# The reciprocal of the softmax row sums on GpSimd, as a power, in front of its multiply

## What is computed

```python
x = x + _L0_xattn_ref(_layernorm(x), ctx_1024, ctx_1024, mask, Wq, bq, Wk, bk, Wv, bv, Wo, bo)
x = x + _L0_ffn_ref(_layernorm(x), w_gate, b_gate, W1, b1, W2, b2)
# inside the attention:
scores = jnp.einsum('bhqd,bhkd->bhqk', q, k) / jnp.sqrt(jnp.float32(DH))
scores = jnp.where(m, -jnp.inf, scores)
attn = jax.nn.softmax(scores, axis=-1)
ctx = jnp.einsum('bhqk,bhkd->bhqd', attn, v)
# inside the experts: the best of 8 experts per token, by a softmax gate
h = jax.nn.relu(jnp.einsum('nd,edm->enm', x_flat, W1) + b1[:, None, :])
y = jnp.einsum('enm,emd->end', h, W2) + b2[:, None, :]
out = y[route_idx, jnp.arange(n)] * route_p[:, None]
```

## Time and profile before

| | |
|---|---|
| median of three runs | 152.0 us (150.82 to 152.23) |
| the profiled execution's own time | 151.69 us |
| its span, first to last instruction | 150.0 us |
| mean granted TensorE clock | 0.876 |
| TensorE busy with matmuls | 110.7 us |
| VectorE busy | 83.6 us |
| ScalarE busy | 71.2 us |
| GpSimd busy | 51.0 us |

### The profile page before, as it was taken

One profiled execution on the slowest core, in us unless ns is written; L12 is line 12 of the kernel. 1 busy time (PEld: TensorE's weight loads), 2 busy tenths in 40 slices (PEclk: granted clock), 3 DMA queues, 4 the chain that ended last, 5 costly groups with the idle time before them and its releaser, 6 DMA issues.

```text
span 150.0 us, 2810 instructions
## 1 busy us (share of the span) xinstructions
PE 110.7 (74%) x753; PEld 87.5 (58%) x753; DVE 83.6 (56%) x292; ACT 71.2 (47%) x355; POOL 51.0 (34%) x82
## 2 busy tenths in 40 slices
PE   5689865997949995989587670848199899898130
PEld 5558644664746574757465560627198699797130
DVE  0340899675523855685668478277172757676010
ACT  0046451416599229782979420313535386466000
POOL 4004075002222332233274543053303615565411
PEclk9999997899996999999999998555559999999655
DMA  4979999999992000000000001101102323200000
GB/s 136 310 244 305 275 271 251 238 255 377 300 283 97 4 0 0 0 2 4 0 20 18 4 0 38 47 26 38 32 5 75 95 54 75 68 20 18 26 0 9
DMA packets 17610, 15.09 MB, mean 101 GB/s; under 512 B 1256, under 2 KB 14756, under 8 KB 17584
## 3 DMA queue, kind: packets, MB, share of 16 engines
q1 hardware_dynamic: 16384, 12.58, 32.9%
q0 software_dynamic: 672, 1.07, 2.2%
q10 hardware_dynamic: 528, 1.14, 2.2%
HBM read 8.92 MB, written 6.19 MB: 101 GB/s over the span
## 4 chain that ended last, share of the span: by engine, by line
PE 51%; DVE 21%; issue 10%; ACT 8%; POOL 4%; DMA 3%; ACTq 0%; DVEq 0%; POOLq 0%
PE bank L865 10%; PE bank L1009 9%; PE bank L877 8%; PE bank L983 6%; ACT probs L696 5%; PE bank L893 4%; PE bank L994 4%; DVE normed L1238 3%; PE bank L960 3%; DMA mask_u<-in_mask_1xSxS_bk 3%; PE bank L946 2%; POOL probs L548 2%; DVE probs_T L1442 2%; PE bank L980 2%; PE bank L851 1%
## 5 line engine op out<-in xcount | busy, mean ns | idle before, releaser
L696 ACT ACTIVATE probs<-bank,neg_max 128x64 f32<-128x64 f32 x120 | 35.6, 376 | 2.3 <-DVE neg_max L1406 2.3
L696 ACT ACTIVATION_READ_ACCUMULATOR probs<-bank,neg_max 128x1 f32 x120 | 30.6, 270 | 0.0
L548 POOL TENSOR_TENSOR probs<-probs,inv_sum 128x512 f32<-128x512 f32 x15 | 15.6, 1041 | 36.4 <-DVE inv_sum L1422 36.3
L1009 PEld LDWEIGHTS bank<-vo,probs_T 128*128 128x128 f32 x128 | 17.1, 205 | 14.5 <-issue 7.3
L1009 PE MATMUL bank<-vo,probs_T 128*128 128x128 f32 x128 | 19.2, 297 | 4.9 <-DVE probs_T L1442 3.5
L641 ACT ACTIVATE w_qkv<-bank,b_stage 128x128 f32<-128x128 f32 x52 | 14.9, 369 | 10.6 <-PE bank L865 10.5
L877 PE MATMUL bank<-w_sb,w_qkv 128*128 x104 | 15.9, 302 | 4.8 <-issue 4.5
L994 PE MATMUL bank<-ident,probs 128*128 128x128 f32 x64 | 10.8, 294 | 10.0 <-POOL probs L548 5.1
L983 PE MATMUL bank<-zero_padded,normed_T 128*128 128x512 f32 x32 | 18.1, 651 | 0.0
L877 PEld LDWEIGHTS bank<-w_sb,w_qkv 128*128 128x128 f32 x104 | 14.2, 212 | 5.2 <-issue 5.2
L590 POOL DMA_INDIRECT out_x<-vo,token_of x10 | 10.0, 999 | 15.4 <-DVE vo L1592 10.6
(11 more groups left out here) (162 smaller groups left out, 193.7 us busy)
## 6 DMA issues: line engine op xcount, KB each, us to landing
regions<-empty_row SPq DMA_DIRECT2D x1, 4224.0 KB, 25.5
w_sb<-in_L_ffn_W SPq DMA_DIRECT2D x1, 2048.0 KB, 27.6
vo<-regions SPq DMA_DIRECT2D x15, 66.0 KB, 1.9
w_qkv<-in_L_xattn_Wk ACTq DMA_DIRECT2D x1, 512.0 KB, 4.2
x_tok<-in_x SPq DMA_DIRECT2D x2, 256.0 KB, 7.2
w_qkv<-in_L_xattn_Wq ACTq DMA_DIRECT2D x1, 512.0 KB, 5.4
w_qkv<-in_L_xattn_Wv SPq DMA_DIRECT2D x1, 512.0 KB, 8.3
wo_sb<-in_L_xattn_Wo SPq DMA_DIRECT2D x1, 512.0 KB, 9.3
```

The lines of the kernel that those rows point to most:

```text
L548: pool.tensor_tensor(p, p, inv, ALU.mult).then_inc(short["normalised"], 1)
L696: last = act.activation(probs[:, n % 2, g, c], score_bank[n % 2][g][:, c], ACT.Exp, bias=neg_max[:, n % 2, g, i:i + 1], accum_out=row_sum[ ...
L1009: last = pe.matmul(out_bank[:, 0:D], probs_T[:, g, k * P:(k + 1) * P], vo[:, (b % 2) * 8 + r * 4 + i, :], start=g == 0 and k == 0, stop=g ...
```

## The change

The reciprocal leaves VectorE. In the short branch GpSimd raises the row sums to the power of minus one, element by element against a constant tile of minus ones, 128x8, and then waits for its own result before the multiply. The wait for the exponentials moves with it to GpSimd. The semaphores keep their names and counts. The last half (7, 1) and the general branch keep VectorE's reciprocal.

```diff
@@ -93,6 +93,7 @@
         ones_bf = sb("ones_bf", [P, P], BF16)
         before = sb("before", [P, P], BF16)
         minus_half = sb("minus_half", [P, NT])
+        minus_one = sb("minus_one", [P, 8])
         falling = sb("falling", [P, QT, E])
         thresholds = sb("thresholds", [1, E, E])
         upto = sb("upto", [1, E, E])
@@ -222,7 +223,7 @@
         router_loaded, experts_loaded = sem("router_loaded"), sem("experts_loaded")
         cleared, consts_made, more_consts = sem("cleared"), sem("consts_made"), sem("more_consts")
         var_ready, rstd_ready, normed_ready, x_bo_ready = map(sem, ("var_ready", "rstd_ready", "normed_ready", "x_bo_ready"))
-        flag_filled = sem("flag_filled")
+        flag_filled, ones_negated = sem("flag_filled"), sem("ones_negated")
         far_min_ready, flag_ready, zeros_ready = sem("far_min_ready"), sem("flag_ready"), sem("zeros_ready")
         dve_done = sem("dve_done")
         x1_ready = sem("x1_ready")
@@ -471,6 +472,7 @@
             pool.memset(ident[:], 0.0).then_inc(cleared, 1)
             pool.memset(ones[:], 1.0).then_inc(consts_made, 1)
             pool.memset(minus_half[:], -0.5).then_inc(consts_made, 1)
+            pool.memset(minus_one[:], -1.0).then_inc(ones_negated, 1)
             pool.wait_ge(cleared, 1)
             pool.affine_select(out=ident[:], in_=ident[:], compare_op=ALU.not_equal, fill=1.0, base=0,
                                pattern=[[-1, P]], channel_multiplier=1).then_inc(consts_made, 1)
@@ -542,6 +544,11 @@
                 for kind, *at in short_steps():
                     if kind == "inverse":
                         n, g = at
+                        if (n, g) == (0, 0):
+                            pool.wait_ge(ones_negated, 1)
+                        pool.wait_ge(short["exp_done"], 2 * n + g + 1)
+                        pool.tensor_tensor(inv_sum[:, n % 2, g, :], row_sum[:, n % 2, g, :], minus_one[:],
+                                           ALU.pow).then_inc(short["inv_ready"], 1)
                         pool.wait_ge(short["inv_ready"], 2 * n + g + 1)
                         p = probs[:, n % 2, g, :].rearrange("p (h w) -> p h w", w=TAIL)
                         inv = inv_sum[:, n % 2, g, :].unsqueeze(2).to_broadcast([P, BANK // TAIL, TAIL])
@@ -1416,10 +1423,6 @@
                         dve.wait_ge(short["vo_filled"], 2 * b + 1)
                         dve.tensor_copy(vo[:, (b % 2) * 8:(b % 2) * 8 + 4, :],
                                         vo_bank[0][:].rearrange("p (k d) -> p k d", d=D)).then_inc(short["vo_vector"], 1)
-                    elif kind == "inverse":
-                        n, g = at
-                        dve.wait_ge(short["exp_done"], 2 * n + g + 1)
-                        dve.reciprocal(inv_sum[:, n % 2, g, :], row_sum[:, n % 2, g, :]).then_inc(short["inv_ready"], 1)
                     elif kind == "center":
                         n, g = at
                         dve.wait_ge(short["max_ready"], 2 * n + g + 1)
```

## The result

| | before | after |
|---|---|---|
| median of the runs, us | 151.41 (4 runs, 150.63 to 152.23) | 158.06 (4 runs, 157.35 to 159.41) |
| profiled execution, us | 151.69 | 158.54 |
| its span, us | 150.0 | 156.8 |
| mean granted TensorE clock | 0.876 | 0.882 |

The ratio is 1.0449, 95% interval 1.0347 to 1.0552: slower by 6.65 us, with 160.9 forecast and a range of 156.2 to 164.6. Counted from the median of 152.0 that it started from, the forecast was +8.9.

What follows compares the result with a forecast made beforehand. No engine is full; the serial exp, reciprocal, multiply, transpose chain at pair restarts bounds the kernel. Median 152.0 plus 7.3 us replayed delay (restarts, then GpSimd's queue) plus 1.6 for the clock gives 160.9 us, range 156.2 to 164.6.

Steps and rivals of the forecast that it cites:

- What bounds the kernel, and the three restarts: Serial exp, reciprocal, multiply, transpose at (1,0), (3,0), (5,0): each hand-over 1.63 us longer, 4.9 us in all.
- the two waits: Semaphore waits added on GpSimd around each power, estimated at 0.1 us each.
- The straight line for the power: GpSimd's power, extended from rows of one, two and four columns at 168 ns a column: 1.72 us for eight.
- the case of a power near 1.05 us: Rival: columns beyond four cost little, replay gives +4.1 us, time 156.1 us; chance 0.06.
- GpSimd as the bound of the last pairs: From (5,0) on, powers and multiplies share GpSimd with row scatters; shift grows from 4.9 to 7.3 us at (6,1).
- The (3,0) transposes "at about 62.9": Sign: TensorE's transposes of (3,0) start at about 62.9 us, from 59.59 and two delays.
- The clock: Longer TensorE idle stretches in the attention bring one more half-clock stretch than now, +1.6 us.
- the two places named: Before (3,0) and (5,0), TensorE's idle stretches become 2.9 us; clock falls expected there.
- the rival without an extra half-clock stretch: TensorE's idle gaps grow but the clock holds: 159.3 us; chance 0.21.
- The shared port: Rival: GpSimd's power and multiply hold up VectorE's gate choice in (3,1) by 1.5 us, once: 162.4 us; chance 0.1.
- VectorE's busy time "down by 3 us": Sign: losing fifteen reciprocals of about 0.2 us cuts VectorE's busy time by 3 us with nothing gained.
- The other side: Rival: eight-column power costs only about 0.41 us and the half-clock stretch at 44 goes: 151.8 us; chance 0.04.

Runs made afterwards that it cites:

- restarts alone: Changed kernel with the power only in (1,0), (3,0), (5,0), VectorE's reciprocal in the other 12 steps: 159.09 us against 151.01 before.
- the reference: Kernel before plus eight small unused GpSimd instructions during an early wait; full clock until after (7,0), 56.29 us from the transposes of (0,0) to those of (7,1).
- the shift at equal clock: Changed kernel with unused TensorE products filling its idle time (154.0 us, ratio 1.0238 to before), its step starts compared with the reference.
- The kernel with the other twelve powers: Changed kernel with the power in 12 steps, VectorE's reciprocal kept in (1,0), (3,0), (5,0): 154.24 us.
- no reciprocal at all, and no meetings: Kernel before without the 15 reciprocals, GpSimd's multiplies of (4,0) and (6,0) also waiting for VectorE's expert choice: 150.06 us, ratio 0.9917.
- the run with late scatters: Changed kernel with the first batch's two row scatters issued behind the multiply of (7,0): 159.76 us against 150.72 before.

## Why the prediction was right, and what was off

- **What bounds the kernel, and the three restarts:** right in the main. A restart costs 1.54 us by idle time (restarts alone) and 1.4 by shift, predicted 1.63. Too high were the power (1.64 for 1.72) and the two waits (0.07 for 0.1). In the first pair the price fell at (0,1), which now waits 1.54 us, and not at (1,0), whose idle time stayed 1.90. In the next pairs (2,1) and (4,1) wait 0.75 us, where the reference has no wait, so the idle times before (3,0) and (5,0) are 2.47 and 2.48 and not the 2.81 of the restarts alone. The steps between had less cover than the prediction gave them; a pair moved by 1.4 us all the same.
- **The straight line for the power:** right, and it holds to 16 columns. The elementwise rule of the GPSIMD Engine Reference in the Trainium skill (section 3.1), which the prediction put beside it, prices the multiply and not the power. With that the case of a power near 1.05 us is out.
- **GpSimd as the bound of the last pairs:** right, the term that the groups alone would not have given. Of the shift at equal clock, 6.7 us, 2.4 come behind (5,0), predicted 2.4. The transposes of (6,1) start at 91.36, predicted 91.4, and that close a hit is in part luck: the shift by the queue was 6.7 there and not 7.3, and 0.4 of clock and 0.2 of a later start filled it up.
- **The (3,0) transposes "at about 62.9"** started at 61.33: the half-clock stretch at 44 us was absent in this execution, which takes 1.4, and the shift was 0.3 smaller (0.2 of a later start goes the other way).
- **The clock, the step that was mis-sized.** There was one stretch more than in before, as forecast, but in part by luck. Of the two places named one had a fall, (3,0); (5,0) had none, and the other fall came behind (6,0), after idle times of 1.27 and 1.34 us. With the restarts alone two idle times of 2.81 us had none. And the price varies: about 1.6 us behind (3,0), 1.4 in before, 0.5 behind (6,0). The prediction's 1.6 compared the 4.11 us from (1,0) to (1,1) with a stretch of step (3,0) that ends at another instruction, the gate's product at 62.06; the same step takes 2.74 us in the reference, which leaves 1.4. The sum: 6.7 + 2.25 - 1.39 = 7.5 us in the stretch; predicted 7.3 + 1.6 = 8.9. The part behind took 0.9 less and the start 0.2 more, which gives the span's 6.8. I count these last two as scatter: the part behind is 55.5 us in the reference too, with the instructions of before. The measured 158.06 lies nearer to the 159.3 of the rival without an extra half-clock stretch than to 160.9, though that stretch did come.
- **The shared port:** half right. In the changed kernel the pair of gate instructions met a multiply once:
```profile
82.88 0.83 DVE L1299 SCALAR_TENSOR_TENSOR candidates<-logits,gate_max,falling 128x8 f32<-128x8 f32 x2
...
77.73 0.14 DVE L1325 TENSOR_TENSOR seen<-seen,onehot 128x8 bf16<-128x8 bf16 x1
77.91 0.16 DVE L1326 TENSOR_TENSOR seen<-seen,onehot 128x8 bf16<-128x8 bf16 x1
```
  The first lies beside the multiply of 82.50 and takes 0.47 us more than usual; the others lie inside the power of 76.54 to 78.18 and take their usual time. The kernel with the other twelve powers has the very two instructions inside a power, that of (5,1):
```profile
74.57 1.67 POOL L552 TENSOR_TENSOR inv_sum<-row_sum,minus_one 128x8 f32<-128x8 f32 x1
...
75.56 0.36 DVE L1304 SCALAR_TENSOR_TENSOR candidates<-logits,gate_max,falling 128x8 f32<-128x8 f32 x2
...
76.17 0.18 DVE L1308 TENSOR_TENSOR onehot<-falling,chosen 128x16 bf16<-128x16 f32 x1
```
  Both take their usual time. The rival's 1.5 us needed the power to hold VectorE up, and it doesn't.
- **VectorE's busy time "down by 3 us"** was wrong: it stayed 83.6. The 15 reciprocals, 2.9 us, had overlapped their neighbours by 0.08 us at most of their ends, some 1.5 us together, and the max and the candidates took 0.3 and 0.5 us more; the rest is not traced.
- **The other side** is out twice: eight columns cost 1.64 us, and even with no reciprocal at all, and no meetings, the stretch gained only 0.3.

## What to carry to other kernels

An idle engine is no free engine: the power was added to an engine that was 34% busy, but its price counts where the chain passes through it, and again where its queue (here the scatters) is full for three steps running. Price an operation by its own kind at two or more sizes, from rows, before you carry an elementwise rule to it. And look at the granted clock before tuning a hand-over: unused products in idle time gave 3.4 us of the kernel's time here, leaving the reciprocal out gave 0.3 us of the stretch.

## What had not been expected of the hardware

A multiply on GpSimd holds up VectorE instructions of 0.17 to 0.36 us until it ends (1.22 and 1.48 us), while a power of 1.64 us with two inputs in the same memory does not: the same two instructions took 0.36 and 0.18 us inside one. Nor does the multiply hold up every VectorE instruction: x1, which has an input in PSUM, took its usual 0.34 us at 73.80 in before, inside the multiply of 73.41 to 74.45. Making GpSimd earlier can therefore cost time: the kernel without any reciprocal had a stretch 1.8 us longer than with it.

Equal idle times of TensorE have no equal consequence for its clock: 2.47 us before (3,0) was followed by half clock, 2.48 before (5,0) was not, and in the run with late scatters it was; 2.81 was not, twice, with the restarts alone; 1.90 before (1,0) was in before and not in the reference or after. What decides between them stays open; no run here separates it.
